# Two edits to an eight-core kernel of layer norm, linear attention and a block-sparse feed-forward: the mask-row loads go from SP's queue to ScalarE's, and the attention stage function is split in two

## The reference

```python
xn = _layernorm(x)                                  # x: (8, 2048, 2048)
q, k, v, u = xn@Wq, xn@Wk, xn@Wv, xn@Wu             # 16 heads of 128
q, k, u = relu(q)/SCALE, relu(k)/SCALE, silu(u)
kv = einsum('bhlk,bhlv->bhkv', k, v)                # no softmax
s = (srms_norm(einsum('bhlk,bhkv->bhlv', q, kv)) * u) @ Wo
mask = top 4 of 16 blocks by softmax(xn @ Wr.T + br), per token
h = gelu(xn @ W1.T) * mask                          # 16 blocks of 512
g = silu(h @ W2.T)
return x + s * g
```

## Time and profile before

| | us |
|---|---|
| two timed runs | 7212.0 and 6948.97 |
| their median | 7080.49 |
| the profiled execution, its own time | 6863.39 |
| span of its slowest core (core 3), first to last instruction | 6861.2 |
| spans of its eight cores | 6806.8 to 6861.2 |
| TensorE matmul busy on core 3 | 3621.3 (53% of the span) |
| ScalarE busy | 1345.2 (20%) |
| VectorE busy | 1147.3 (17%) |
| GpSimd busy | 481.3 (7%) |
| first and last mask-row DMA issued, at | 1304.8 and 4270.7 |

### The profile page before, as it was taken

One profiled execution on the slowest core, in us unless ns is written; L12 is line 12 of the kernel. 1 busy time (PEld: TensorE's weight loads), 2 busy tenths in 40 slices (PEclk: granted clock), 3 DMA queues, 4 the chain that ended last, 5 costly groups with the idle time before them and its releaser, 6 DMA issues.

```text
span 6861.2 us, 48930 instructions; the slowest of 8 cores (6806.8 to 6861.2 us)
## 1 busy us (share of the span) xinstructions
PE 3621.3 (53%) x15250; PEld 1491.6 (22%) x15250; DVE 1147.3 (17%) x1750; ACT 1345.2 (20%) x1923; POOL 481.3 (7%) x747
## 2 busy tenths in 40 slices
PE   2223676766656676565657666644343443434444
PEld 1111333322222232222223222211111111111111
DVE  3342000011111111110111111112322322230000
ACT  2222111122222222222222222221111111110000
POOL 0000000000000000000000000000000001002222
PEclk9999888988888888788888878866666665657777
DMA  1001111122232222323322232320000000003343
GB/s 38 31 31 56 50 49 43 37 86 86 86 98 87 84 80 88 117 86 98 88 84 83 83 82 84 86 74 25 18 19 25 13 25 25 13 12 93 102 98 100
DMA packets 154605, 439.66 MB, mean 64 GB/s; under 512 B 23232, under 2 KB 23232, under 8 KB 150256
## 3 DMA queue, kind: packets, MB, share of 16 engines
q1 hardware_dynamic: 103424, 251.77, 12.2%
q0 software_dynamic: 50928, 184.75, 9.7%
HBM read 402.82 MB, written 33.55 MB: 64 GB/s over the span
## 4 chain that ended last, share of the span: by engine, by line
PE 41%; DMA 26%; ACT 11%; DVE 10%; issue 9%; POOL 2%; ACTq 1%; DVEq 0%; POOLq 0%; SPq 0%
PE hps L423 15%; DMA w2ring<-w2t 12%; PE yps L456 7%; DMA gst<-gscr 4%; PE qp L531 4%; PE kp L322 3%; PE qp L540 3%; DVE srow L585 3%; PE vp L327 3%; ACT w2b L446 2%; ACT w1b L414 2%; ACT hm L427 2%; PE bcp L590 2%; DMA wring<-wur 2%; DMA wring<-wqr 2%
## 5 line engine op out<-in xcount | busy, mean ns | idle before, releaser
L456 PE MATMUL yps<-w2b,hm 128*128 128x512 bf16 x4096 | 950.0, 397 | 701.7 <-ACT w2b L446 701.7
L423 PE MATMUL hps<-A,w1b 128*128 128x512 bf16 x4096 | 1014.7, 411 | 341.2 <-ACT w1b L414 341.2
L456 PEld LDWEIGHTS yps<-w2b,hm 128*128 128x128 bf16 x4096 | 413.2, 101 | 1238.4 <-issue 797.6
L423 PEld LDWEIGHTS hps<-A,w1b 128*128 128x128 bf16 x4096 | 418.3, 104 | 937.9 <-issue 548.9
L644 PE MATMUL sps<-wob,osb 128*128 128x512 bf16 x1024 | 298.4, 459 | 369.6 <-ACT wob L630 197.7
L446 ACT CAST w2b<-w2ring 128x512 bf16<-128x512 f32 x512 | 316.2, 618 | 837.9 <-DMA w2ring<-w2t 832.3
L465 DVE TENSOR_TENSOR y_acc<-y_acc,yps 128x1024 f32<-128x1024 f32 x224 | 273.6, 1221 | 1165.9 <-PE yps L456 1165.9
L531 PE MATMUL qp<-A,wqb 128*128 128x512 bf16 x1024 | 261.9, 424 | 390.9 <-ACT wub L518 390.9
L442 POOL DMA_DIRECT2D w2ring<-w2t x256 | 137.3, 536 | 3724.6 <-ACT w2b L446 3709.0
L590 PE MATMUL bcp<-srow,onesrfs 1*128 1x512 f32 x128 | 130.6, 1122 | 405.3 <-DVE srow L585 405.3
L431 DVE TENSOR_TENSOR hm<-hm,mbc 128x1024 bf16<-128x1024 bf16 x128 | 88.6, 692 | 1428.1 <-ACT hm L427 1428.1
(11 more groups left out here) (92 smaller groups left out, 2298.1 us busy)
## 6 DMA issues: line engine op xcount, KB each, us to landing
w1ring<-w1r SPq DMA_DIRECT2D x256, 512.0 KB, 4.6
w2ring<-w2t SPq DMA_DIRECT2D x256, 256.0 KB, 3.3
w2ring<-w2t POOLq DMA_DIRECT2D x256, 256.0 KB, 3.5
xtile<-x POOLq DMA_DIRECT2D x16, 1024.0 KB, 5.1
wring<-wk SPq DMA_DIRECT2D x64, 256.0 KB, 3.8
wring<-wv SPq DMA_DIRECT2D x64, 256.0 KB, 3.9
gscr<-y_acc POOLq DMA_DIRECT2D x16, 1024.0 KB, 8.4
wring<-wqr POOLq DMA_DIRECT2D x64, 256.0 KB, 3.5
```

The lines of the kernel that those rows point to most:

```text
L423: p.e("tensor", lambda e, i=i, ii=ii, ng=ng, sl=sl, hf=hf, tok0=tok0: e.matmul(hps[sl][:, ng * 512:(ng + 1) * 512], w1b[hf][:, ii * 128:(i ...
L456: p.e("tensor", lambda e, t8=t8, jc=jc, fg=fg, fh=fh, sl=sl: e.matmul(yps[sl][:, fg * 512:(fg + 1) * 512], hm[:, jc * 1024 + t8 * 128: jc ...
```

## The change

The first edit makes the four mask-row DMAs of each slab ScalarE's, with the two waits that go with them and with a set of four semaphores of their own, `dV`, in place of `dS`. The second divides `stage_attn` into `attn_mms` (the four matmuls and their copies) and `ssbc` (the normalization), and calls `ssbc(h - 2)` ahead of `stage_qu(h)`.

```diff
+    dV = p.dsem("dV")
...
                 for gg in range(2):
-                    p.w("sync", cS, mask_done[NT - 1])
-                    p.w("sync", cT, mrow_guard[0])
-                    mrow_dma = p.dma("sync", lambda e, ...: e.dma_start(out=mrow[0:1, :], in_=maskT[...]), dS)
+                    p.w("scalar", cS, mask_done[NT - 1])
+                    p.w("scalar", cT, mrow_guard[0])
+                    mrow_dma = p.dma("scalar", lambda e, ...: e.dma_start(out=mrow[0:1, :], in_=maskT[...]), dV)
                     p.wd("tensor", mrow_dma)
...
-    def stage_attn(h):
+    def attn_mms(h):
...
             attn_evac[ng] = p.v(cV)
+
+    def ssbc(h):
+        par = h % 2
         for hh2 in range(2):
...
     for h in range(NH):
+        if h >= 2:
+            ssbc(h - 2)
         stage_qu(h)
         if h >= 1:
-            stage_attn(h - 1)
-    stage_attn(NH - 1)
+            attn_mms(h - 1)
+    ssbc(NH - 2)
+    attn_mms(NH - 1)
+    ssbc(NH - 1)
```

More of the change, by code:

```diff
@@ L393, in build @@
                 for gg in range(2):
-                    p.w("sync", cS, mask_done[NT - 1])
-                    p.w("sync", cT, mrow_guard[0])
-                    mrow_dma = p.dma("sync", lambda e, b=b, gg=gg, tok0=tok0: e.dma_start(out=mrow[0:1, :], in_=maskT[b:b + 1, tok0 + gg * 512: tok0 + (gg + 1) * 512]), dS)
+                    p.w("scalar", cS, mask_done[NT - 1])
+                    p.w("scalar", cT, mrow_guard[0])
+                    mrow_dma = p.dma("scalar", lambda e, b=b, gg=gg, tok0=tok0: e.dma_start(out=mrow[0:1, :], in_=maskT[b:b + 1, tok0 + gg * 512: tok0 + (gg + 1) * 512]), dV)
                     p.wd("tensor", mrow_dma)
```

## The result

The changed kernel takes 6914.17 us (median of 35 runs), the kernel before 6920.41 us (median of 34 runs measured beside it). The ratio is 1.0047 with a 95% interval of 1.0025 to 1.0069: the change makes the kernel slower by about 32 us (0.0047 x 6870; by the interval 17 to 47). The forecast was 6 us faster. The time itself lies in the stated range, but the sign was wrong, and this is the thing to explain.

The account below looks back on a forecast made before the run. It took waits handed between engines as the bound, with three small DMA round trips between slabs. Terms -27.3 - 2.0 + 8.5 + 8 + 7 gave -5.8 us, so 7008 became 7002 us; range 6845 to 7200, change -30 to +45.

Parts of the forecast that it names:

- Attention edit: Attention stage: splitting the function leaves every engine's order of instructions the same; cost 0, gain 0, with no range.
- (a): Start of each slab: W1 loads issue earlier on SP, so ScalarE's wait for them goes; gain 27.3 us in total.
- (b): First slab: the first mask row arrives in time, so TensorE waits only for VectorE's last copy; gain 2.0 us.
- (c): Other slabs: first mask-row DMA goes out later, behind the last W2 cast, covered by TensorE's product; cost 0.
- (d): Second and fourth mask-row DMAs wait for the matmul before, on ScalarE as on SP; same price if landing times match.
- (e): Third mask-row DMA, behind the first mbc copy on ScalarE, may wait for its end; cost 8.5 us, between 0 and 17.
- (f): Early W1 pair in flight while the second half's W2 ring fills, delaying casts; cost 8 us, from 0 to 38.
- (g): Change of token half: mask rows stand behind the Silu activations and meet POOL's stores; cost 7 us once, 0 to 10.
- estimate of 14 us at most: Limit on (f) if queues take turns by packet: a W2 load loses at most its transfer time, about 0.87 us.
- The clock: First chunks of each slab: a shorter gap ahead might move 1.8 us either way per slab, 29 us in all.
- Rival 1: Overlap of W1 pair and W2 loads costs more than the removed wait: net +33 to +36, 7044 us; chance 0.15.
- Rival 3: ScalarE's DMA queue is slower for small loads, 3.8 us against 1.7: 101 us more, 7103 us; chance 0.07.

Follow-up runs that it names:

- e1: Kernel before with only the attention function split, mask rows staying on SP: ratio 1.0004, slab 195.07 us.
- e4: Changed kernel (mask rows on ScalarE), W1 pair held until the last W2 cast of the slab before: ratio 0.9987, slab 195.32 us.
- e6: Kernel before, mask rows on SP, W1 pair issued ahead of them but held until the last W2 cast: slab 195.93 us, no ratio.
- e7: e4 with the W1 pair held only until the first half's 16 W2 casts are done: slab 198.79 us, no ratio.
- e2: Mask-row edit alone, with SP issuing a slab's first W1 pair only after the third broadcast matmul: ratio 1.0062, slab 197.25 us.
- e5: e4 plus a needless 1.4 us ScalarE copy ahead of each slab's first W1 cast: ratio 1.0028, slab 195.49 us.
- e12: e4 plus a needless ScalarE copy of 600 elements ahead of the first W1 cast: slab 195.61 us, no ratio.
- e11: Kernel before plus the needless 1.4 us ScalarE copy ahead of the first W1 cast: slab 196.84 us, no ratio.
- e3: Kernel before, mask rows on SP, next slab's W1 pair issued early, ahead of the mask rows: ratio 1.0018, slab 197.61 us.

## Why the prediction was wrong, by its own steps

The forecast was -6 us in the sum, and 36.8 us were lost up to the last slab. The term by term account, with 16 slabs:

- **Attention edit**, 0: right (e1, 1.0004).
- **(a)**, -27.3: right; the wait went, 1.52 us a slab, 24 us.
- **(b)**, -2.0: half right. The first broadcast now waits for VectorE's last copy only (it comes at 1302.9 us in the mean of the eight cores, at 1304.5 before), but the second, issued together with the W1 pair, waits 5.15 us for its row. The first slab is 2.0 us longer in all, no more than an ordinary one. The timeline of its first two broadcasts, after:

```profile
1308.27 0.37 PE L399 MATMUL hps<-mrow,onesrbs 1*128 1x512 bf16 x1 [1.23 <-DVE kvsb L348]
...
1313.79 0.58 PE L399 MATMUL hps<-mrow,onesrbs 1*128 1x512 bf16 x1 [5.15 <-DMA mrow<-maskT]
```

- **(c)**, 0: right; the row is issued at 1671.56 and is wanted at 1702.61. **(d)**: right in kind, ScalarE's rows land in 1.7 us like SP's. The changed kernel's row of issues:

```profile
mrow<-maskT ACTq DMA_DIRECT2D x64, 1.0 KB, 1.7
```

- **(e)**, 8.5 between 0 and 17: near the low end. The issue doesn't wait for the copy; that step is 0.20 us longer, all three together 0.31 (e4 against e6: 0.23), so 4 to 5 us. The Trainium skill, "Perfetto Trace Analysis", section "DVE / Act Engine Instruction (TENSOR_ADD, Activation, etc)", had it right: the DMA goes out 0.19 us after the copy's start.
- **(f)**, 8, at most 38: this is the step that failed. Measured are 2.0 us a slab counted from the last Gelu (32 us), or 1.6 us counted from cast 13 (25 us). The prediction asked only what happens to the loads of the second half, and for the 16 casts of that half its 0.5 us a slab is what they lost (0.49, 8 us). The other 1.50 us are lost in the first half, and for them it had no term: the last W2 loads of the first half stand ahead of the pair in SP's queue, and it put their loss at nothing without a reason. The last of them lands 1.0 us later. The lead of 2.9 us did not protect the first load of the second half either; it lands 1.4 us later, though its cast comes behind the late 16th one and the half loses only the 0.49.
- The estimate of 14 us at most that the prediction worked out beside (f), from the Trainium skill, "DMA: Bandwidth & Descriptors", section "Queues, rings and completion order", is of the second half alone, and the 8 us there lie within it. For the single load it does not hold: 0.87 us was to be the most that one could lose, and 1.4 us were lost here and 2.8 us in e7. Of loads on the pair's own queue, where most was lost, it says nothing.
- **(g)**, 7: right in size. The two slabs around the change of token half take 413.8 us together before and 423.4 after, +9.6, of which 4.2 are the two ordinary losses, so 5.4. The first mask row waits for the stores as foreseen, and the second for another 5.15:

```profile
2908.47 8.21 ACTq L397 DMA_DIRECT2D mrow<-maskT  x2
...
2915.47 0.58 PE L399 MATMUL hps<-mrow,onesrbs 1*128 1x512 bf16 x1 [24.00 <-DMA mrow<-maskT]
...
2921.19 0.58 PE L399 MATMUL hps<-mrow,onesrbs 1*128 1x512 bf16 x1 [5.15 <-DMA mrow<-maskT]
...
2928.19 2.18 ACT L415 CAST w1b<-w1ring 128x1024 bf16<-128x1024 f32 x2
```

- **The clock**, left at 0 with 29 us either way: this was the second failure. It took back 1.29 us a slab (83.09 against 81.80), 21 us. The prediction had seen the two lengths of a chunk in rows 3 and the shorter gap, and had no reason for a sign. The one trace gave me none.

Together: -24 + 5 + 32 + 21 + 5 is +39. Measured are 36.8 to the start of the last slab, that is over 15 slabs; with the four terms that come in every slab (34 together) cut by a sixteenth, the sum is 37.

Rival 1, that the overlap costs more than the wait it removes, came out with its sign, and its +36 is near the +32 measured. That is partly luck: it had (e) at 17 us, which is 5, and no clock, which is 21. Rival 3 is excluded, ScalarE's small loads are as fast as SP's. Had I taken 1.6 us a slab for (f) and changed nothing else, the forecast would have been +12.

## What to carry to other kernels

Moving a transfer to an idle time of the consumer is no gain if at that time a ring of short loads is what the kernel waits for; look at what else is in flight when the load lands, ahead of it in its own queue too, and hold it until the ring is done. A wait of one or two microseconds ahead of a matmul burst may be worth nothing, because slower chunks behind it give it back; try a pad in its place before you work on it. And where a ring of two buffers sets the pace, a third and fourth are worth far more than the order of the queues.

## What the runs showed of the hardware

- A 1 KB load released together with two of 512 KB on another queue kept TensorE waiting 4.5 us in place of 1.9 (e2).
- 256 KB loads were slowed by 512 KB loads issued after them on the same queue: the last of 16 landed in 4.42 us against 3.37, in the mean of 96. The first load on GpSimd's queue behind them landed in 5.02 us against 3.65.
- A useless 1.4 us copy on the path cost 0.2 us a slab at most, since the chunks behind it ran 1.5 us faster (e5 against e4). The dependence on the whole hand-over is not steady: 83.1, 82.0, 81.6 and 82.4 us of chunks for hand-overs of 10.3, 11.2, 11.8 and 12.8 us (e4, e12, e5, e11).
- In eight bursts of 32 matmuls, one to each chunk of 9.7 to 11.0 us, every second one had the lower mean clock (before and after: 0.86 to 0.91 against 0.96 to 0.98, chunk 0 aside), and which ones they were went with the length of the hand-over ahead of them (even ones before, at 11.5 us; odd ones after, at 10.3 us, and in e11, at 12.8 us).
- In the kernels with overlap (the change, e3, e7) the W2 casts are already 0.4 to 0.6 us later at cast 13 than the mean of the others (25.5 us), before the core's own W1 pair is out. But e6, which has no early pair, is 0.4 us later than that mean too, so it may be scatter. This stays open, as does the reason why the clock alternates.
